# New keys of an attention layer: turned on TensorE before they are stored, or by the DMA that loads them

## What is computed

```python
q = einsum('bsd,ed->bse', x, Wq).reshape(B, S, 32, 128)      # B = 64, S = 32, width 512
k = einsum('bsd,ed->bse', x, Wk).reshape(B, S, 8, 128)
v = einsum('bsd,ed->bse', x, Wv).reshape(B, S, 8, 128)
q = rope(rmsnorm(q, q_norm_w), pos);  k = rope(rmsnorm(k, k_norm_w), pos)
k_all = concatenate([k_cache[block_table], k], axis=1)       # 512 cached tokens and 32 new ones
v_all = concatenate([v_cache[block_table], v], axis=1)
scores = where(valid, einsum('bqhd,bkhd->bhqk', q, repeat(k_all)) * SCALE, -1e30)
o = einsum('bhqk,bkhd->bqhd', softmax(scores), repeat(v_all))
x = x + einsum('bse,de->bsd', o.reshape(B, S, 4096), Wo)
```

## Time and profile before

| | |
|---|---|
| median of 3 runs | 2138.39 us (2136.91 to 2140.44) |
| the profiled execution's own time | 2135.74 us |
| its span in the profile | 2134.0 us |
| TensorE (matmul) busy | 2064.6 us, 97% |
| VectorE, ScalarE, GpSimd busy | 79%, 69%, 52% |
| TensorE's granted clock | 0.99 of full speed |
| DMA queue of SyncE | 57.8% of the 16 DMA engines' time, 375.65 MB |

### The profile page before, as it was taken

The page is one execution under the profiler, slowest core; times in us unless marked ns, Lnnn a source line. Parts: engine busy times, 40 slices in busy tenths (PEclk is TensorE's granted clock), DMA queues, the critical chain, the costliest instruction groups (busy, mean ns, idle before and its releaser), DMA issues.

```text
span 2134.0 us, 55706 instructions
## 1 busy us (share of the span) xinstructions
PE 2064.6 (97%) x17214; PEld 1346.9 (63%) x17214; DVE 1676.1 (79%) x4282; ACT 1475.1 (69%) x4204; POOL 1103.1 (52%) x1856
## 2 busy tenths in 40 slices
PE   7889999999999888999999999999999999999999
PEld 4444555555555456667777777777777777777775
DVE  6897888888887677777777777777777777777774
ACT  3457777777777666667777777777777777777774
POOL 5456656565666545444545454545454545454542
PEclk9999999999999989999999999999999999999999
DMA  7856777786677588988888888888888888888881
GB/s 279 268 211 173 241 235 239 236 237 194 222 231 249 191 289 281 302 246 257 247 258 246 252 247 259 243 250 253 246 253 252 252 248 249 252 254 245 250 244 55
DMA packets 416041, 514.10 MB, mean 241 GB/s; under 512 B 67299, under 2 KB 313955, under 8 KB 413188
## 3 DMA queue, kind: packets, MB, share of 16 engines
q1 hardware_dynamic: 378292, 375.65, 57.8%
q0 software_dynamic: 37456, 134.89, 19.6%
HBM read 413.90 MB, written 92.54 MB: 237 GB/s over the span
## 4 chain that ended last, share of the span: by engine, by line
PE 57%; DVE 3%; SPq 2%; issue 1%; DMA 1%; ACT 0%; DVEq 0%; POOL 0%; ACTq 0%; POOLq 0%
PE att_scores L1679 15%; PE att_y L1729 14%; PE att_tr L1688 10%; PE att_o L1715 5%; PE att_o L1716 5%; PE att_o L1717 5%; DVE att_prob L1832 1%; PE att_tr_new L1694 1%; PE att_o L1718 1%; PE att_scores L1680 1%; SPq L131 1%; SPq L125 1%; DVE att_mask L1815 1%; DMA att_keys<-k_parts 1%; DVE att_tpl L1856 0%
## 5 line engine op out<-in xcount | busy, mean ns | idle before, releaser
L1832 DVE CUSTOM_DVE_ANT_0 att_prob<-att_scores,att_mask 128x544 f32<-128x544 f32 x512 | 370.7, 724 | 294.1 <-PE att_scores L1680 290.5
L1758 ACT ACTIVATE att_tph<-att_tr 128x512 f16<-128x512 f32 x512 | 305.9, 597 | 329.8 <-PE att_tr L1688 328.3
L1628 POOL CAST att_parts<-att_norm 128x96 f16<-128x96 f32 x512 | 135.4, 264 | 563.5 <-issue 556.7
L1729 PE MATMUL att_y<-att_wo,att_ot 128*128 128x512 f16 x1536 | 407.7, 379 | 0.0
L1856 DVE TENSOR_TENSOR att_tpl<-att_tr,att_tph 128x512 f16<-128x512 f32 x512 | 349.9, 683 | 0.4 <-ACT att_tph L1758 0.2
L1688 PE MATMUL att_tr<-ident,att_norm 128*128 128x128 f32 x2048 | 326.2, 282 | 0.0
L1267 POOL TENSOR_TENSOR proj_rn<-proj_ra,proj_rb 128x512 f32<-128x512 f32 x128 | 190.4, 1487 | 197.5 <-DVE proj_rb L1381 162.9
L1715 PE MATMUL att_o<-att_tph,att_values 128*128 128x128 f16 x1536 | 284.6, 220 | 2.4 <-ACT att_of L1758 2.0
L1717 PE MATMUL att_o<-att_tph,att_values 128*128 128x128 f16 x1536 | 284.5, 220 | 0.0
L1716 PE MATMUL att_o<-att_tpl,att_values 128*128 128x128 f16 x1536 | 284.5, 220 | 0.0
L1688 PEld LDWEIGHTS att_tr<-ident,att_norm 128*128 128x128 f32 x2048 | 215.9, 141 | 61.8 <-issue 1.1
(11 more groups left out here) (227 smaller groups left out, 5305.3 us busy)
## 6 DMA issues: line engine op xcount, KB each, us to landing
room<-k_parts SPq DMA_DIRECT2D x512, 128.0 KB, 2.7
att_keys<-k_parts SPq DMA_DIRECT2D x512, 128.0 KB
q_parts<-proj_turned SPq DMA_DIRECT2D x128, 256.0 KB, 3.6
v_new_parts<-proj_vp SPq DMA_DIRECT2D x64, 256.0 KB, 3.2
room<-q_parts SPq DMA_DIRECT2D x32, 512.0 KB, 7.2
att_query<-q_parts SPq DMA_DIRECT2D x32, 512.0 KB
w<-in_w_t SPq DMA_DIRECT2D x12, 1024.0 KB, 7.6
room<-in_k_t SPq DMA_DIRECT2D x8, 1024.0 KB, 7.7
```

The lines of the kernel that those rows point to most:

```text
L1729: last = mm(y_ps[:, :], ot[p][:, a, h, :], wo[:, h, w, :], start=(h == 0 and start), stop=(h == HQ - 1 and stop))
L1758: copy = lambda out, in_, **kw: nc.scalar.activation(out, in_, ACT.Copy, **kw)
L1832: v.tensor_tensor_reduce(out=prob[q][:, :], in0=sc[q], in1=mask[bi % 2][:, at:at + LK], scale=1.0, scalar=-3.0e38, op0=ALU.add, op1=ALU.ma ...
```

## The change

Keys are no longer turned on TensorE. ScalarE and VectorE split the normalised rows of `kr` directly into high and low parts, the store writes them row by row into `kn_d`, now of shape (2048 rows, 2048 values), and `load_sample` reads the 32 rows of a sample with a transposing DMA. Semaphore counts follow: `heads_turned` counts queries alone, ScalarE's `heads_high` for keys waits for the normalised keys, and GpSimd's add into `kr` waits until the low parts of the tile before were made. `held` is the same wait on the two `tq` banks, counted without the keys.

```diff
 def load_sample(nc, sp, b, t, bi, keys, query, row_scale, page_row, k_d, kn_d, q_d, rs_d, loaded):
-    sp.dma_start(keys[:, NPP].rearrange("p h two s -> p (h two s)"),
-                 kn_d[ds(b, 1)].rearrange("o p m -> (o p) m")).then_inc(loaded, 16)
+    sp.dma_start(keys[:, NPP].rearrange("p h two s -> p (h two) s"), kn_d[ds(b * S, S), :], transpose=True
+                 ).then_inc(loaded, 16)
...
-    kn_d = nc.dram_tensor("k_new_parts", (B, P, PG), F16).ap()
+    kn_d = nc.dram_tensor("k_new_parts", (B * S, HK * 2 * HD), F16).ap()
...
-            src = tq[n % 2][:, :].rearrange("p (h b s) -> p b h s", h=HB, b=BT)
-            dst = buf[:, :].rearrange("p (b h two s) -> p b h two s", b=BT, two=2, h=HB)
-            return src, dst[:, :, :, 0], dst[:, :, :, 1]
+            src = kr[n - QB][:, :].rearrange("p (h c) -> p h c", h=HB)
+            dst = buf[:, :].rearrange("p (h two c) -> p h two c", two=2, h=HB)
+            return src, dst[:, :, 0], dst[:, :, 1]
...
-                    w = PG // KB
-                    dst = kn_d[ds(t * BT, BT), :, (n - QB) * w:(n - QB + 1) * w].rearrange("b p c -> p b c")
-                    src = src.rearrange("p (b c) -> p b c", b=BT)
+                    dst = kn_d[ds(t * P, P), (n - QB) * 2 * D:(n - QB + 1) * 2 * D]
...
             def turn_heads(t, n):
                 idx = t * ROT + n
-                if n < QB:
-                    pe.wait_ge(sum_done, idx + 1)
-                    src = rn[n % NR]
-                else:
-                    pe.wait_ge(kn_done, t * KB + n - QB + 1)
-                    src = kr[n - QB]
-                after(pe, high, idx - 1)
-                after(pe, low, idx - 1)
+                pe.wait_ge(sum_done, idx + 1)
+                src = rn[n % NR]
+
+                held = idx - 1 if n >= 2 else idx - 1 - KB
+                after(pe, high, held)
+                after(pe, low, held)
...
-                    if heads_at(t, n):
+                    if heads_at(t, n) and heads_at(t, n)[1] < QB:
                         turn_heads(*heads_at(t, n))
...
-            for n in range(QB, ROT):
-                turn_heads(NT - 1, n)
...
-                act.wait_ge(tq_done, idx + 1)
+                if n < QB:
+                    act.wait_ge(tq_done, t * QB + n + 1)
+                else:
+                    act.wait_ge(kn_done, t * KB + n - QB + 1)
...
                 if n >= QB:
-                    after(pool, tq_done, (t - 1) * ROT + n + 1)
+                    after(pool, low, (t - 1) * ROT + n + 1)
```

More of the change, by code:

```diff
@@ L1258, in add @@
                 if n >= QB:
-                    after(pool, tq_done, (t - 1) * ROT + n + 1)
+                    after(pool, low, (t - 1) * ROT + n + 1)
                     out = kr[n - QB]
                 elif n >= NR:
-                    pool.wait_ge(tq_done, t * ROT + n - NR + 1)
+                    pool.wait_ge(tq_done, t * QB + n - NR + 1)
                     out = rn[n % NR]
                 else:
-                    after(pool, tq_done, (t - 1) * ROT + n + QB - NR + 1)
+                    after(pool, tq_done, (t - 1) * QB + n + QB - NR + 1)
                     out = rn[n % NR]
```

## The result

| | before | changed |
|---|---|---|
| median of 5 runs, taken in turns | 2140.44 us (2136.91 to 2142.62) | 2153.62 us (2151.96 to 2160.23) |
| profiled execution, its own time | 2135.74 us | 2154.83 us |
| its span | 2134.0 us | 2153.1 us |

The ratio of the runs, taken by their means, is 1.0070, with a 95% interval of 1.0055 to 1.0084: 15 us slower (13 us by the medians), where 8.65 us faster was forecast. The time lies outside the range of the prediction.

The account below looks back on a forecast made before the run. TensorE was taken to bound the projections and long attention stretch, sample loads the early stretch. 13.05 + 0.3 - 4.7 = 8.65 us faster, so 2138.39 - 8.65 = 2129.7 us, range 2124.0 to 2137.0.

Parts of the forecast that it names:

- The transposes that go: Projections, TensorE: dropping the key transposes saves 0.87 us a tile, 13.05 us over 15 tiles.
- Who is late next?: Projections: block 4 waits for VectorE's reading of block 0, with 5.2 us left, so nobody delays TensorE.
- I cost that at nothing: Projections: ScalarE and VectorE read keys from SBUF instead of PSUM at no cost; even a tenth of a microsecond each stays hidden.
- Rival 4: Projections: transposes go but the pace stays, ScalarE or VectorE being behind at a tile's turn; 2142.8 us, chance 0.03.
- Rival 2: Early attention: the load becomes the bound and the kernel slower, 25.9 us paid at the far bound; 2150.9 us, chance 0.08.
- The tail: End of the projections: the last store's issue stays behind the value stores, its landing shrinks by 0 to 0.7 us, 0.3 taken.
- The load's issue: Head of each sample's load, SyncE's queue: a transposing issue takes 1.27 us against 0.34, so 0.93 us more.
- The load's part on the DMA engines: Each sample's load: the transposing transfer takes the DMA engines 0 to 0.36 us more than the direct one.
- The sum of 4.7 us: Early attention: dearer loads cost 3.7 us for four waited samples plus 1.0 us for the other three.
- Which samples pay: Early attention: samples 2, 3, 5 and 8 pay in full, three others 1.0 us together; steady samples pay nothing.
- a sign of being wrong: First scores of samples 2 to 8: waits should grow from 9.05 to about 14 us; shrinking would refute the prediction.
- rival 3: Early attention: longer waits drop TensorE's clock, about 2 to 3 us each at samples 5 and 8; 2134.7 us, chance 0.11.

Follow-up runs that it names:

- pool_low: The changed kernel with the low parts of the key blocks made by GpSimd instead of VectorE; 2132.89 us against 2137.67 for before, ratio 0.9988.
- psum_low: The changed kernel, but VectorE's low parts of keys take one source from a zero-filled PSUM bank; 2136.56 us against 2137.67 for before, ratio 0.9994.
- pool_low_last: pool_low with the transposing load of new keys issued behind its sample's queries, scales and pages; 2133.84 us, ratio to before 0.9975.
- proj_turn: pool_low with stored key blocks turned in the projections by SBUF-to-SBUF transposing transfers, and loaded plainly in attention; 2245.53 us, ratio to before 1.0497.

## Why the prediction was wrong

- **The transposes that go** were sized right: 0.44 us a block, with the pitch of 2.59 us in every tile, the changed kernel's too, and 13.1 us in the sum where nobody was late (pool_low, without its tile 13). The last matmul of the projections came 7.4 us later, not 13 earlier.
- **"Who is late next?"** is the step that failed first. It looked at one bank, block 4 against VectorE's reading of block 0, with 5.2 us to spare. The thin place was the other pair of banks: the turn of query block 2 against the rest of block 0, with 1.9 us, in the same tile of the same trace. That turn was late once before the change, by 0.35 us in tile 0.
- **"I cost that at nothing"** is the step that decided it. It gave ScalarE and VectorE the same duration for a source in SBUF as for one in PSUM, with a tenth of a microsecond as its bound. VectorE's half costs 1.08 us for one of two blocks of a tile, and small instructions behind it (L110, L112) went from 0.45 and 0.78 to 0.93 and 1.22 us. That took the whole gain of 13 us and 5.7 more; psum_low, with this one source back in PSUM, has 13.9 us of it again. No row with this form was looked for, though the trace of before has it: there L110 and L112, with 128x1 operands, already take 0.45 and 0.60 to 0.85 us, up to the end of GpSimd's add.
- **Rival 4**, a pace that stays since VectorE is behind, was the one nearest to the mechanism in the projections, at a chance of 0.03, though it named neither the bank nor why VectorE is behind. Its time, 2142.8, was too mild: the stage got 5.7 us longer.
- **Rival 2** gave 2150.9 us, near the 2153.62 measured, but by luck: it put 25.9 us on the early stretch, which got 10.5 longer, and took the 13 us of the projections as won.
- **The tail** was right: the stores still stand behind the four of the values, and it is 0.2 us shorter, for 0.3 predicted. SyncE's queue in the changed kernel:

```profile
749.41 1.87 SPq L981 DMA_DIRECT2D v_new_parts<-proj_vp  x4
751.38 0.40 SPq L973 DMA_DIRECT2D k_new_parts<-proj_turned  x1
```

- **The load's issue** was right in size (1.22 to 1.46 us for the eight of the early stretch). As the cause it is doubtful: moved to the end in pool_low_last, it won next to nothing. How much of the 8 us it carries is open.
- **The load's part on the DMA engines** was the mis-sized term, at 0 to 0.36 us, of which the sum used none. It was read off a transpose from SBUF in the projections, where the DMA engines are at 0.76, and the hole of 0.35 us in the earlier trace rows is seven slices, of which five are at 51 to 67 GB/s. In the early stretch, at 0.95, the rate lies under 110 GB/s for about 1 us and more. The sum of 4.7 us became about 8 over the profiles, 10.5 in the one of the changed kernel.
- **Which samples pay** was half right. Waits rose to 16.7 us (14 expected), but 12.2 of them at the values, which the prediction didn't look at since they are on another queue. At the first scores, where it looked, they fell from 9.05 to 4.50 us, which it had named as a sign of being wrong. The steady stretch hides nearly all of the load: two samples waited, 1.0 us together, where it said none would.
- **The clock** (rival 3) was part of it: 3.8 of the 10.5 us are longer busy time at a granted clock of 0.93 for 0.95, near the 5 us that the rival gave. No run holds the clock still, so this is read from the windows and not tested.

## What to carry to other kernels

When an operand moves from PSUM to SBUF, list what VectorE and GpSimd run side by side before costing it at nothing: a short instruction can take the length of the other engine's. Ask for the slack of every pair of buffers that the sped-up engine writes, and take the thinnest. A DMA that costs little alone is priced where the DMA engines are full, by what everybody else doesn't move in the meantime; if it is dear only in one stretch, let that stretch keep the old way.

## What the runs showed of the hardware

- VectorE with two SBUF sources and GpSimd, reading SBUF, exclude each other for a whole instruction: 0.68 us becomes 1.76, and even 128x1 operands wait (0.93 and 1.23 us).
- A transposing DMA of 128 KB from DRAM in packets under 512 bytes costs 1.24 us of issue at the median of the changed kernel's 64 (plain 0.34), and beside DMA engines busy at 0.95 is followed by 1 to some 4 us in which all of them together move under 110 GB/s, for 270 on the mean. The Trainium skill has transposing DMAs as fast as ordinary ones ("Advanced Engine Details and Errata", section X-Bar Transpose (TRN2)). In the steady stretch the time nearly agrees with that (about 1 us for 55 loads); in the early one the measurement differs, by about 1 us a load, and decides.
- The issue of a transposing DMA didn't shrink with its size: 1.25 us at the median for 1024 columns of 32 rows from SBUF (128 in proj_turn) as for 2048 from DRAM. A single one of the changed kernel, that of sample 0, took 0.58.
